# Feed-forward weights rounded and compared beside the batches instead of in a stage ahead of them

## The reference

```python
def _tlin(x, w, s):
    return jnp.einsum('bsi,oi->bso', x, w) * s
h = jax.nn.silu(_tlin(x, w1_w, w1_s)) * _tlin(x, w2_w, w2_s)
h = jax.nn.gelu(_tlin(h, h1_w, h1_s), approximate=False)
h = jax.nn.gelu(_tlin(h, h2_w, h2_s), approximate=False)
return _tlin(h, w3_w, w3_s)
...
x = x + _L0_attn_ref(xn, ...) + _L0_ffn_ref(xn, ...)
xn = _layernorm(x, axis=-1)
x = x + _L1_attn_ref(xn, ...) + _L1_ffn_ref(xn, ...)
```

## Time and profile before

| | |
|---|---|
| median of 3 runs | 2233.71 us (2226.56 to 2234.21) |
| the profiled execution | 2224.04 us, its span 2222.4 us |
| TensorE busy in the span | 1757.2 us (79%) |
| VectorE, ScalarE, GpSimd busy | 51%, 46%, 45% |
| feed-forward, first to last instruction | about 507 to 1266 us in the span |

### The profile page before, as it was taken

One profiled execution on the slowest core, in us unless ns is written; L12 is line 12 of the kernel. 1 busy time (PEld: TensorE's weight loads), 2 busy tenths in 40 slices (PEclk: granted clock), 3 DMA queues, 4 the chain that ended last, 5 costly groups with the idle time before them and its releaser, 6 DMA issues. The chain is left out here.

```text
span 2222.4 us, 33910 instructions
## 1 busy us (share of the span) xinstructions
PE 1757.2 (79%) x10759; PEld 1099.7 (49%) x10759; DVE 1127.4 (51%) x2401; ACT 1024.4 (46%) x1356; POOL 1007.0 (45%) x778
## 2 busy tenths in 40 slices
PE   3889889870599999999999738877888888747933
PEld 2455555540487787787787513333433433235510
DVE  4666666537513313313313248877787788447211
ACT  1555555543313322223223118887787888713400
POOL 2443444430234344333433308777687777724212
PEclk8999999985799999999999868999998999969965
DMA  3333333306201101101100153222222222043989
GB/s 103 96 96 94 96 95 91 95 11 211 77 1 47 47 0 47 47 0 47 35 12 28 57 198 93 69 71 71 81 67 76 85 63 52 10 177 141 357 306 329
DMA packets 129732, 204.38 MB, mean 92 GB/s; under 512 B 14303, under 2 KB 84063, under 8 KB 129668
## 3 DMA queue, kind: packets, MB, share of 16 engines
q1 hardware_dynamic: 107896, 163.40, 24.7%
q10 hardware_dynamic: 16096, 20.65, 2.6%
q0 software_dynamic: 5680, 19.57, 2.3%
HBM read 95.96 MB, written 56.69 MB: 69 GB/s over the span
## 5 line engine op out<-in xcount | busy, mean ns | idle before, releaser
L773 POOL TENSOR_TENSOR l_prob<-l_prob,l_bias 128x1024 f32<-128x1024 f32 x192 | 452.3, 2376 | 145.5 <-ACT l_prob L881 144.6
L1336 POOL TENSOR_TENSOR f_hl<-f_full,f_hh 128x512 fp32r<-128x512 f32 x192 | 248.1, 1292 | 439.4 <-DVE f_hh L1378 282.9
L946 DVE CUSTOM_DVE_ANT_0 l_slot<-l_slot,l_bias 128x512 f32<-128x512 f32 x512 | 340.4, 714 | 51.5 <-PE l_slot L1020 50.4
L1378 DVE CAST f_hh<-f_full 128x512 fp32r<-128x512 f32 x128 | 74.9, 585 | 397.7 <-ACT f_full L1357 396.2
L884 ACT ACTIVATE l_prob<-l_prob 128x1024 f32<-128x1024 f32 x256 | 271.0, 1070 | 0.0
L1422 PE MATMUL f_ps<-f_hh,f_hi_h 128*128 128x512 f32 x1024 | 267.1, 397 | 0.0
L1432 PE MATMUL f_ps<-f_hl,f_hi_h 128*128 128x512 f32 x1024 | 265.8, 396 | 0.0
L451 DVE TENSOR_REDUCE l_peak<-l_slot 128x2 f32<-128x256 f32 (+3 forms) x256 | 206.3, 821 | 110.8 <-PE l_slot L535 108.5
L1357 ACT ACTIVATE f_full<-f_ps,f_h_s 128x512 f32<-128x512 f32 x128 | 86.4, 688 | 332.5 <-PE f_ps L1432 308.7
L376 ACT ACTIVATE l_prob<-l_slot 128x1024 f32<-128x1024 f32 (+3 forms) x256 | 174.7, 706 | 95.0 <-PE l_slot L554 91.9
L1422 PEld LDWEIGHTS f_ps<-f_hh,f_hi_h 128*128 128x128 f32 x1024 | 192.8, 188 | 49.3 <-ACT f_hh L1350 2.6
(11 more groups left out here) (211 smaller groups left out, 2655.0 us busy)
## 6 DMA issues: line engine op xcount, KB each, us to landing
l_stacks<-l_parts SPq DMA_DIRECT2D x384, 128.0 KB, 2.7
inter<-e_stage POOLq DMA_DIRECT2D x32, 512.0 KB, 5.1
c_rows<-inter SPq DMA_DIRECT2D x32, 512.0 KB, 9.7
attn<-l_out_sb ACTq DMA_DIRECT2D x16, 512.0 KB, 2.8
f_raw<-in_L_ffn_h_w SPq DMA_DIRECT2D x16, 512.0 KB, 3.3
e_w<-in_L_ffn_f SPq DMA_DIRECT2D x32, 256.0 KB, 4.8
l_bias<-ext ACTq DMA_DIRECT2D x16, 448.0 KB, 12.3
l_x_in<-in_L_attn_x SPq DMA_DIRECT2D x8, 512.0 KB, 3.8
```

Of the source, the lines that this page charges most:

```text
L773: return eng.tensor_tensor(probs(n), src, bias[:, h:h + 2, j * P:j * P + T], ALU.add)
L946: ins = dve.tensor_tensor_reduce(src, src, bias[:, 4 * g + 2 * pr + a, t * P:t * P + T], 1.0, 3 * NEG, ALU.add, ALU.max, peak[:, g, a, pr, ...
L1336: pool.tensor_tensor(hl[layer % 2][:, o], full[:, n % 2], hh[layer % 2][:, o].bitcast(F32), ALU.subtract).then_inc(h_lo.sem, 1)
```

## The change

The setup block is gone. The blocks of weights (`BLOCKS`, 22 of 512 KB: halves of w1 and w2 by columns, rows of h1 and h2 by 128, halves of w3) are loaded into a ring of two places and rounded by ScalarE beside batch 0 (`make`): four ahead of it, one after each tile of the gate layer and of h1, the last two at the end of h1. TensorE waits at the start of a layer of each batch until its weights are there (`parts_there`, `needs`). All 8 batches run without low parts of the weights and without branches.

The comparison goes beside the batches' h2 layer: batch i loads one eighth of each matrix again, as seven pieces of 128 or 256 KB (`PIECES`), ScalarE rounds each (`round_piece`), VectorE compares it twice (`compare`). After the last batch the flag is made. Then a second block would make the low parts and run all batches a second time with them, if the flag were 1. The bias table is made after the last batch; its loads and its store are issued by ScalarE. `Layers` holds the engines' streams for one batch; its text is that of before, with `parts_there` and `beside` called in it.

```diff
+        CH, HALF = 1024, HID // 2
+        raw = sb("raw", [P, 2, CH])
...
+        BLOCKS = [(m, half) for half in range(2) for m in ("w1", "w2")] + [(m, k) for m in ("h1", "h2") for k in range(KH)] + \
+                 [("w3", half) for half in range(2)]
+        PIECES = (("w1", 0), ("w2", 0), ("w3", 0), ("h1", 0), ("h1", 1), ("h2", 0), ("h2", 1))
...
+        needs = {("gate", 0): 2, ("gate", 1): 4, ("h1", 0): 4 + KH, ("h2", 0): 4 + 2 * KH, ("w3", 0): len(BLOCKS)}
+        def parts_there(pe, what, half):
+            pe.wait_ge(made.sem, needs[what, half])
...
-                for n, (m, k) in enumerate(chunks):
-                    if n >= RING:
-                        sp.wait_ge(compared.sem, n - RING + 1)
-                    sp.dma_start(raw[:, n % RING, 0:wide[m]], w[m + "_w"][k * P:(k + 1) * P])\
-                      .then_inc(loaded[n % RING].sem, 16)
...
+                def load_block(n):
+                    if n >= 2:
+                        sp.wait_ge(made.sem, n - 1)
+                    sp.dma_start(block_raw(n), block_of(n)[0]).then_inc(block_in[n % 2].sem, 16)
+                def pieces(i):
+                    for u in range(len(PIECES)):
+                        src, wide_, parts = piece_of(u, i)
+                        if u >= 2:
+                            sp.wait_ge(compared.sem, compared.at(2 * (u - 1), i))
+                        dst = raw[:, u % 2, 0:wide_]
+                        if parts > 1:
+                            dst = dst.rearrange("p (k n) -> p k n", k=parts)
+                        sp.dma_start(dst, src).then_inc(piece_in[u % 2].sem, 16)
+                def store(b):
+                    sp.wait_ge(f.out_done.sem, f.out_done.at(2, b))
+                    sp.dma_start(out_d[b].rearrange("(t p) d -> p t d", p=P), t.out_sb[:]).then_inc(f.out_saved.sem, 16)
+                load(0)
+                for n in range(4):
+                    load_block(n)
+                load_sums(0)
+                for n in range(4, len(BLOCKS)):
+                    load_block(n)
+                sp.wait_ge(made.sem, len(BLOCKS))
+                with sp.Fori(0, B - 1) as i:
+                    sp.wait_ge(f.gu_ps.sem, f.gu_ps.at(KH, i))
+                    load(i + 1)
+                    pieces(i)
+                    store(i)
+                    load_sums(i + 1)
+                pieces(B - 1)
+                store(B - 1)
+                sp.wait_ge(f.out_saved.sem, f.out_saved.at(1, B - 1))
...
-                table.move(pool)
...
+                def make(n):
+                    act.wait_ge(block_in[n % 2].sem, 16 * (n // 2 + 1))
+                    act.activation(block_of(n)[1], block_raw(n), ACT.Copy).then_inc(made.sem, 1)
+                def make_beside(n):
+                    if n < KH:
+                        make(4 + n)
+                    elif n < 2 * KH:
+                        make(4 + n)
+                        if n == 2 * KH - 1:
+                            make(5 + n)
+                            make(6 + n)
+                    else:
+                        round_piece(0, n)
+                def round_piece(i, n):
+                    for u in ((0, 1), (2,), (3,), (4,), (5,), (6,), (), ())[n - 2 * KH]:
+                        act.wait_ge(piece_in[u % 2].sem, piece_in[u % 2].at(u // 2 + 1, i))
+                        act.wait_ge(compared.sem, compared.at(2 * u, i))
+                        wide_ = piece_of(u, 0)[1]
+                        act.activation(rounded[:, 0:wide_], raw[:, u % 2, 0:wide_], ACT.Copy).then_inc(p_rounded.sem, 1)
+                for n in range(4):
+                    make(n)
+                act.wait_ge(s_done.sem, 2)
+                f.act_batch(act, 0, t, make_beside)
+                with act.Fori(1, B) as i:
+                    f.act_batch(act, i, t, lambda n: round_piece(i, n) if n >= 2 * KH else None)
+                table.load(act)
+                table.copies(act)
+                table.store(act)
+                act.wait_ge(table.saved, 16)
...
-                    pair = raw[:, n % RING, 0:wide[m]], hi[m][:, k].bitcast(F32)
-                    for sign in range(2):
-                        ins = dve.tensor_tensor_reduce(junk[:, sign, 0:wide[m]], pair[sign], pair[1 - sign], 1.0, 0.0,
-                                                       ALU.subtract, ALU.max, peaks[:, sign, n:n + 1])
-                    ins.then_inc(compared.sem, 1)
...
+                def compare(i, n):
+                    for u in ((0, 1), (2,), (3,), (4,), (5,), (6,), (), ())[n - 2 * KH]:
+                        wide_ = piece_of(u, 0)[1]
+                        dve.wait_ge(p_rounded.sem, p_rounded.at(u + 1, i))
+                        dve.wait_ge(compared.sem, compared.at(2 * u, i))
+                        if u == 0:
+                            dve.wait_ge(worst_done.sem, worst_done.at(0, i))
+                        pair = raw[:, u % 2, 0:wide_], rounded[:, 0:wide_].bitcast(F32)
+                        for sign in range(2):
+                            if sign:
+                                dve.wait_ge(compared.sem, compared.at(2 * u + 1, i))
+                            dve.sem_inc(held.sem, 1)
+                            dve.tensor_tensor_reduce(junk[:, 0:wide_], pair[sign], pair[1 - sign], 1.0, 0.0,
+                                                     ALU.subtract, ALU.max, peaks[:, sign, u:u + 1]).then_inc(compared.sem, 1)
+                    if n == 3 * KH - 2:
+                        dve.wait_ge(compared.sem, compared.at(2 * len(PIECES), i))
+                        dve.wait_ge(worst_done.sem, worst_done.at(0, i))
+                        dve.tensor_tensor(worst[:], worst[:], peaks[:], ALU.max).then_inc(worst_done.sem, 1)
+                with dve.Fori(0, B) as i:
+                    f.dve_batch(dve, i, t, lambda n: compare(i, n) if n >= 2 * KH else None)
...
+                dve.tensor_scalar(flag[:], top_of[:], 0.0, None, ALU.is_gt).then_inc(found.sem, 1)
+                dve.wait_ge(found.sem, 3)
...
+                with pe.Fori(0, B) as i:
...
                 table.products(pe)
...
-                any_low = pe.value_load(flag[0:1, 0:1], min_val=0, max_val=1)
...
-                        with pe.If(any_low == 1):
-                            for s in range(2):
-                                pe.wait_ge(lo_in[s].sem, lo_in[s].at(o + 1, i))
-                            products(two, [[(low[:, s, k], xh[:, k]) for k in range(KD)] for s in range(2)],
-                                     False, False).then_inc(lo_used.sem, 2)
...
+                with pe.If(pe.value_load(flag[0:1, 0:1], min_val=0, max_val=1) == 1):
+                    with pe.Fori(0, B) as i:
+                        g.pe_batch(pe, i, t, all_there)
+        clear(nc, f.tallies)
```

More of the change, by code:

```diff
@@ L1162, in ffn @@
[L1162 to L1171 removed]
+        t = Tiles()
@@ L1231, in ffn @@
-        with nc.sbuf_tensor("f_raw2", [P, 2, CH], F32) as raw, nc.sbuf_tensor("f_lo", [P, 2, CH], F32) as lo, \
-             nc.Block() as block:
+                pe.wait_ge(found.sem, 1)
+                pe.transpose(psum[0][0:1, 0:P], worst_of[:], ident[:]).then_inc(worst_ps.sem, 1)
+        g = Layers(nc, FULL_PASS, "g", True)
+        lo_made, raw_in, saved = g.sem("lo_made"), [g.sem(f"raw_in{j}", unit=16) for j in range(2)], \
+            [g.sem(f"lo_saved{j}", unit=16) for j in range(2)]
@@ new lines, in ffn, with slot, nothing, all_there @@
+        chunks = [(m, k) for m in names for k in range(deep[m])]
+        STREAM = [(m, o) for o in range(KH) for m in ("w1", "w2")] + [("h1", o) for o in range(KH)] + \
+                 [("h2", o) for o in range(KH)] + [("w3", 0)]
+        lo_raw, lo = (t.x_in, t.attn), (t.tanh, t.gated)
+        def slot(tiles, n, m):
+            return tiles[n % 2][:].rearrange("p a b -> p (a b)")[:, 0:wide[m]]
+        def nothing(n):
+            pass
+        def all_there(pe, what, half):
+            pass
@@ L1233, in _ @@
+        with nc.Block() as block:
             @block.sync
@@ L1389, in _ @@
+                        dve.tensor_tensor(slot(lo, n, m), slot(lo_raw, n, m), t.hi[m][:, k].bitcast(F32), ALU.subtract)\
+                           .then_inc(lo_made.sem, 1)
+                    with dve.Fori(0, B) as i:
+                        g.dve_batch(dve, i, t, nothing)
             @block.tensor
             def _(pe):
[L1391 to L1399 removed]
```

554 lines of the change are left out of this document (279 added, 275 removed).

## The result

The changed kernel takes 2197.89 us, the median of 4 runs (2189.94 to 2202.27), beside 2230.14 (2222.91 to 2234.21) for the kernel before on the same chip: ratio 0.9848, 95% interval 0.9817 to 0.9879, a gain of 32 us. The prediction was 2184 with a range of 2170 to 2200. The median lies in the range, near its upper end, and on the side given 0.92, but the gain is 15 us smaller than the sum of 47.6.

The account below looks back on a forecast made before the run. TensorE bounds the steady part, VectorE's comparisons the 72.7 us start. Terms -63.9 + 7.3 + 1.0 + 2.1 + 2.6 + 3.3 = -47.6 give 2176.4 from the profiled execution, 2186.1 from the median; forecast 2184, range 2170 to 2200.

Parts of the forecast that it names:

- the side given 0.92: Whole kernel: faster by more than 0.5% (11 us), chances 0.72 + 0.13 + 0.07.
- Step 1, the start: Stage start: TensorE begins at 516.0 instead of 579.86, once block 1 is made; -63.9 us.
- Step 2, the gate layer: Batch 0's gate layer: ScalarE also makes blocks, 2.45 us a tile, so 25.8 us instead of 18.5; +7.3.
- the first rival, the ring of two: Batch 0's gate layer: blocks land in 5.9 us, one every 3.5, 10 us more; gain 37, 2195; chance 0.13.
- the added 1.0 for the clock: Start of h1 in batch 0: TensorE at a lower clock after waiting; +1.0 us (0 to 3).
- Step 3, the last block of h2: Batch 0 between h1 and h2: TensorE waits for block 19, made behind h1's last Gelu; +2.1 us (1.8 to 3).
- Step 4, the comparison: Each batch's h2 layer: VectorE's comparisons take 8.1 us and ScalarE's roundings 3.7, hidden from TensorE; 0 in each of 8 batches.
- The rival that every comparison is stretched: Each batch's h2 layer: GpSimd stretches comparisons 3.5 times, 10 us a batch, 80 in all, 2264; chance 0.04.
- The steady part: Batch to batch: 85.0 us as before, TensorE at over 98%, removed branches worth 0.
- Step 5, the end: After the last batch: table's products, copy and store +2.6 us, block that reads the flag and skips +3.3 (2.5 to 5).
- the 0.8 for the small product and its copy: After the last batch: estimated 0.8 us for the table's small product and its copy, before the store's issue.
- a skip of over 5 us: Before the next stage: if skipping the second pass costs more than 5 us, the prediction is wrong; it expected 3.3.

## Why the prediction was right, and where its sum was off

**Step 1, the start.** Right: -62.7 against -63.9. The rounding of block 0 began 7.2 us after the first load.

**Step 2, the gate layer.** Right in kind: +10.1 against +8.3, inside its own bounds. What was off in the profiled execution is "lands 3.3 later": block 3 landed 5.5 us after its issue, the blocks of h1 in 4.3, and this, not ScalarE's 2.45 us a tile, made the rhythm (2.72). But the landing varies: with the branches put back it was 3.2 and the rhythm 2.23, below the 2.45 of the sum. So the first rival, the ring of two, was partly true, in some executions, with 4.3 us a load instead of its 5.9, and in all of them at the first blocks: four places bring the start to h1 to 31.8 us, against 35.3 to 39.5 in the traces with two and the waits unchanged. Of the added 1.0 for the clock: the matmuls behind the 4.15 us wait took 3.32 us for seven, 1.97 in a later batch, and the granted clock from 548 to 580 was 0.95.

**Step 3, the last block of h2.** The wait is 1.90 us, predicted 2.1. What was not in the sum is the slow clock behind it: seven matmuls in 3.00 us. Where the same wait of 1.90 was followed by seven in 1.88 (four places) h1 to batch 1 was 69.6, 1.8 over before, the wait alone. The clock granted from 582 to 585 was 0.58 in the first case, and 1.00 from 571.5 to 580 in the second; what decides between them is open. Over steps 2 and 3 the forecast (18.74 + 8.3 + 67.82 + 2.1 = 97.0 us) lies in the 95.5 to 101.3 of the kernels with the same code here.

**Step 4, the comparison.** Right: nothing reaches TensorE, with or without it. The estimate of 8.1 us of VectorE for fourteen reductions was low: the seven first ones of a batch alone take 7.4, 1.06 each, where the sum had 0.69 and 0.42. The Trainium skill (GPSIMD Engine Reference, Key points) says that an instruction with two SBUF inputs contends with GpSimd. The trace agrees. But at most one reduction in each pair pays, six of seven in the batch looked at, and not every one, as the prediction argued from the cast of the earlier trace rows. The rival that every comparison is stretched fell with the tripled ones. The point from which it would cost was put too high: "TensorE asks for that Gelu's bank only four tiles later" and a lateness that "is gone before the out products" forgot that the output layer needs the layer's last cast at once. By the tripled comparisons the estimate is that it costs from 3.7 us a piece on, 0.55 above what is used.

**The steady part.** The prediction had 0 and it was -3.7. The change moved a 4-byte tensor from ahead of the layers' tiles to behind them. Put back, it takes the 3.7 us back. The prediction counted instructions and never looked at where tiles lie.

**Step 5, the end.** Here the sum failed, by 14.8 us, nearly all of its error of 16.6. The failing step is the clause that the table's loads "have most of those products' time and are there". The load of 101 rows took over 19 us on ScalarE's queue. In the kernel before, the same load stood on GpSimd's queue, and the view of DMA issues from 505 to 560 had its landing, which the prediction didn't look up:

```profile
t_fir<-c_fir POOLq DMA_DIRECT2D x1, 404.0 KB, 8.2
```

With the load split, the end is 13.99 us against a forecast of 8.13 + 5.9 = 14.0. Two errors of size cancel in that, which is luck: the table's tail costs 0.8 (13.99 against 13.20) and not 2.6, and the rest, 13.20 - 8.13 = 5.1, is the block that reads the flag, 5.5 by the run without it, and not 3.3. No row stood behind the 0.8 for the small product and its copy. x's last store took 2.8 us, and 2.9 in the kernel before, where the sum had 3.3 from another batch's. The prediction named a skip of over 5 us as a sign of being wrong, and by the 5.1 to 5.5 that sign came, though the time stayed in the range.

The Trainium skill (DMA: Bandwidth & Descriptors, section Why a DMA increments its semaphore by 16 and not by 1) has the rule that the prediction missed: a transfer is spread over the largest number of engines up to 16 that divides the slowest dimension of both of its sides. 101 is prime, so it gets one. For GpSimd's software queue it names an exception, some direct copies whose rows are dealt out in sixteenths, rounded up. The traces agree: a busy share of one engine, some 26 GB/s and 19 us on ScalarE's queue, 8.2 us on GpSimd's, no wait with 96 and 5 rows. x's store, whose last sixteenth landed with the load, fits too: with the load split it took 2.8 us.

**The time itself.** 2184 against 2197.9: the 16.6 us of the stage, less 1.5 for the base (2184 + 47.6 = 2231.6 against the median of 2230.1) and 1.3 between the medians' gain (32.3) and the stage's (31.0). That the time lies in the range is in part luck: the 3.7 us of the moved tensor were not foreseen, and without them the median would be 2201.6, outside.

## What to carry to other kernels

When a DMA moves to another engine's queue, look up how long that very load took before, and how its outermost dimension divides: a load of a prime number of rows may run on one DMA engine, as this one of 101 did, and hold up the stores beside it; cut it into 96 and the rest. When work is put beside a loop, compare its rhythm with one tile of the bound engine. Slack from spare banks doesn't help work that delays a layer's last output. And when a version of the same instruction stream is some tenths of a per cent faster everywhere, look at the addresses.

## What the runs showed of the hardware

- A load of 404 KB in 101 rows ran at some 26 GB/s on ScalarE's queue, with 0.07 of the 16 DMA engines busy, and a 512 KB store issued 8 us behind it took 10.2 us instead of 2.8: 33 of its 528 packets came late.
- 4 bytes ahead of the layers' tiles made a batch 85.00 instead of 84.48 us, 0.6%, with equal instructions. Groups of eight matmuls of 512 columns took 2.03 to 2.04 us instead of 2.02.
- A VectorE instruction with two inputs in SBUF that starts beside a GpSimd subtraction can take 1.3 us with 256 or 512 columns (0.42 and 0.69 alone). It ended 0.3 us (256) or 0.56 us (512) behind the end of GpSimd's, and the next ones were free.
- A block of code that reads a flag and is jumped over cost 5.5 us on the way to the next stage. From flag to next load it was 3.3 where that block was shorter.
- Nearly the same wait of 1.90 to 1.93 us was followed by full speed in some executions (seven matmuls in 1.88, 1.89 and 1.91 us) and by 2.37 to 3.02 us in others, at a granted clock of 0.58 in the first 3 us of one of them.
